# Two attention layers on one core: a head norm moved to DVE, another order in the first batches, and the last batch's value projections in the score banks

## What is computed

```python
def _L0_cond_ref(x, mask, Wq, Wo):
    q = jnp.transpose(x, (0, 2, 1)) @ Wq.T
    qh = q.reshape(B, T, NH, dk).transpose(0, 2, 1, 3)
    scores = scale * jnp.einsum('bhqd,bhkd->bhqk', qh, qh)
    logits = (scores * cmask + (1.0 - cmask) * NEG) * rmask
    ctx = jnp.einsum('bhqk,bhkd->bhqd', jax.nn.softmax(logits, axis=-1), qh)
    return jnp.transpose(ctx.transpose(0, 2, 1, 3).reshape(B, T, D) @ Wo.T, (0, 2, 1))
...
def _L1_cond_ref(x, emb, W_emb, b_emb, g_norm, W_qkv, g_q, g_k, W_out):
    scale, shift = jnp.split(emb @ W_emb + b_emb, 2, axis=-1)
    xn = _rms_norm(x, g_norm) * (1.0 + scale) + shift
    q, k, v = heads(xn @ W_qkv)
    q, k = _rms_norm(q, g_q), _rms_norm(k, g_k)
    attn = jax.nn.softmax(jnp.einsum('bhqd,bhkd->bhqk', q, k) * d ** (-0.5), axis=-1)
    o = merge(jnp.einsum('bhqk,bhkd->bhqd', attn, v))
    return o + o @ W_out
x = x + _L0_cond_ref(x, cond_2048, L0_cond_Wq, L0_cond_Wo)
x = x + _L1_cond_ref(x, cond_2048[:, None, :], ...)
```

## Time and profile before

| what | value |
|---|---|
| three runs, median (lowest to highest) | 1290.88 us (1289.24 to 1292.41) |
| the profiled execution, its own time | 1290.69 us |
| its span, first to last instruction | 1288.5 us |
| mean granted TensorE clock | 0.981 |
| busy: PE, DVE, POOL, ACT | 1231.0, 1032.1, 771.6, 768.5 us |

### The profile page before, as it was taken

One profiled execution on the slowest core, in us unless ns is written; L12 is line 12 of the kernel. 1 busy time (PEld: TensorE's weight loads), 2 busy tenths in 40 slices (PEclk: granted clock), 3 DMA queues, 4 the chain that ended last, 5 costly groups with the idle time before them and its releaser, 6 DMA issues.

```text
span 1288.5 us, 20732 instructions
## 1 busy us (share of the span) xinstructions
PE 1231.0 (96%) x6769; PEld 577.5 (45%) x6769; DVE 1032.1 (80%) x920; ACT 768.5 (60%) x1394; POOL 771.6 (60%) x387
## 2 busy tenths in 40 slices
PE   3889899999999999999999999999999999999998
PEld 1364444545444454544445454444544444454434
DVE  6666878788887878888787888878888897887664
ACT  1616566766656576665657656565766656566524
POOL 1517566484756748575574857557485755837542
PEclk7969999999999999999999999999999999999999
DMA  5712635435373543536354353635345363533432
GB/s 143 266 34 75 155 92 123 110 88 125 82 171 92 120 111 83 133 82 168 95 117 110 87 132 82 163 97 116 95 102 138 82 161 93 119 91 74 98 73 59
DMA packets 77975, 143.00 MB, mean 111 GB/s; under 512 B 21552, under 2 KB 23088, under 8 KB 77872
## 3 DMA queue, kind: packets, MB, share of 16 engines
q1 hardware_dynamic: 69552, 130.36, 40.5%
q10 hardware_dynamic: 8320, 11.32, 3.3%
HBM read 32.02 MB, written 8.39 MB: 31 GB/s over the span
## 4 chain that ended last, share of the span: by engine, by line
PE 80%; POOL 6%; DVE 4%; issue 3%; ACT 3%; SPq 2%; DMA 1%; ACTq 1%; DVEq 0%; POOLq 0%
PE PX L599 25%; PE PS L501 9%; PE PO L531 8%; PE PX L633 8%; PE PS L518 5%; PE PO L553 5%; POOL RQK L2272 4%; PE PM L464 4%; PE PX L570 2%; PE PM L570 2%; PE PO L556 2%; PE PM L473 2%; SPq L2453 2%; PE PM L542 1%; PE PM L581 1%
## 5 line engine op out<-in xcount | busy, mean ns | idle before, releaser
L1213 ACT ACTIVATE E<-PS,KBIAS 128x512 f32<-128x512 f32 x512 | 340.8, 686 | 195.8 <-PE PS L501 152.6
L599 PE MATMUL PX<-WQKV,XNT 128*128 128x512 f32 x752 | 377.2, 604 | 0.7 <-DVE XNT L1895 0.4
L1822 DVE TENSOR_REDUCE NM<-PM 128x4 f32<-128x2048 f32 x128 | 292.1, 2282 | 72.3 <-PE PM L464 72.3
L2260 POOL TENSOR_TENSOR E<-E 128x1024 f32<-128x1024 f32 x112 | 263.3, 2370 | 88.1 <-PE PO L531 77.8
L501 PE MATMUL PS<-B,A 97*128 97x512 f32 x512 | 287.5, 597 | 4.6 <-ACT E L1213 3.8
L2290 POOL TENSOR_TENSOR KQLO<-E 128x1024 f32<-128x1024 f32 x64 | 151.6, 2368 | 224.4 <-ACT E L1220 222.7
L2272 POOL TENSOR_TENSOR RQK<-RQK,HALF 128x16 f32<-128x16 f32 x64 | 212.8, 3331 | 94.7 <-DVE RQK L1910 94.3
L1220 ACT ACTIVATE E<-PS 128x512 f32<-128x512 f32 x256 | 146.9, 597 | 110.6 <-PE PS L518 110.4
L599 PEld LDWEIGHTS PX<-WQKV,XNT 128*128 128x128 f32 x752 | 134.0, 191 | 99.7 <-issue 89.7
L1829 DVE TENSOR_REDUCE NM<-PM 128x8 f32<-128x2048 f32 x64 | 146.3, 2286 | 37.1 <-PE PM L473 37.1
L501 PEld LDWEIGHTS PS<-B,A 97*128 97x128 f32 x512 | 92.2, 189 | 156.5 <-issue 105.2
(11 more groups left out here) (87 smaller groups left out, 1352.4 us busy)
## 6 DMA issues: line engine op xcount, KB each, us to landing
A<-KQHI SPq DMA_DIRECT2D x126, 128.0 KB, 2.4
B<-KQHI SPq DMA_DIRECT2D x126, 128.0 KB, 2.4
A<-QHI SPq DMA_DIRECT2D x248, 64.0 KB, 2.0
B<-QHI SPq DMA_DIRECT2D x248, 64.0 KB, 2.0
XB<-x SPq DMA_DIRECT2D x16, 512.0 KB, 4.1
X<-x ACTq DMA_DIRECT2D x16, 512.0 KB, 5.0
out<-X1R SPq DMA_DIRECT2D x32, 256.0 KB, 2.9
A<-KQLO SPq DMA_DIRECT2D x63, 128.0 KB, 2.4
```

The source lines that it names most:

```text
L599: last = mm(bank, XNT[:, c, t * P:(t + 1) * P], WQKV[:, c, part * DM:(part + 1) * DM], start=(c == 0), stop=(c == 3))
L1213: fn(E[:, probs(seg, i, g), h, :], PS[n % 2][:, :], ACT.Exp, bias=KBIAS[:, g, b:b + 1], scale=SCALE).then_inc(exp_done, 1)
L1822: v.tensor_reduce(NM0[:, q, :].rearrange("p (h k) -> p h k", k=KB0)[:, :, kb], PM[:, :, :], axis=AX.X, op=ALU.max, negate=True).then_inc(m ...
L2260: g_.tensor_tensor(running(seg, i)[:, heads_, :], running(seg, i)[:, heads_, :], E[:, probs(seg, i, g), heads_, :], ALU.add).then_inc(done, 1)
```

## The change

It has three parts. (1) In the steady iterations DVE does the norm of head block 1, between its fourth maximum of layer 0 and an add of exponentials; POOL's list loses it. (2) In the fill, TensorE computes batch 0's first two scores ahead of the second maxima group and the next batch's first projection behind the third; near its end the fourth maxima group of batch 1 goes ahead of the output projection, on TensorE and DVE; and the normalized rows are transposed ahead of batch 1's values, with ScalarE's modulation ahead of its value copy. (3) In iteration 16 the value projections go to the banks PS1 and PS0, counted by a new semaphore `values_taken`, and are spread between transposes and maxima; the rest of the output matmuls go between the scores. ScalarE copies both value tiles before the first exponential, and issues the second half of the maxima rows after two exponentials instead of four. DVE's second residual goes behind the last maximum.

```diff
@@ BIG[16], MAXES[0]
-            (("w1", 0), -2, 0), (("w1", 1), -2, 0), (("v1", 0), -1, 0), (("v1", 1), -1, 0)),
+            (("w1", 0), -2, 0), (("w1", 1), -2, 0)),
...
+        def last_values_bank(t):
+
+            return PS[SCORES.upto(("C", t), NB) % 2]
@@ score1
                 if b == NB - 1:
+                    if u < 2:
+                        pe.wait_ge(values_taken, u + 1)
@@ values_and_sums1
                 if c == 0:
-                    pe.wait_ge(big_taken, BIG.upto(("v1", 1), i))
+                    if b == NB - 1:
+                        pe.wait_ge(values_taken, 2)
+                    else:
+                        pe.wait_ge(big_taken, BIG.upto(("v1", 1), i))
@@ project1
-                bank = heads_bank(i - 1, k) if key[0] == "p1" else PX[:, :]
+                late = key[0] == "v1" and i == NB
+                bank = last_values_bank(t)[:, :] if late else heads_bank(i - 1, k) if key[0] == "p1" else PX[:, :]
                 if cs[0] == 0:
-                    if key[0] == "p1" and i == NB and k % 2:
+                    if late:
+                        pe.wait_ge(exp_done, SCORES.ahead(("C", 0), i))
+                    elif key[0] == "p1" and i == NB and k % 2:
@@ TensorE, iterations_0_and_1
                 maxima0(i, i, 1, 0)
+                score0("A", i, i, 0, 0, 0)
+                score0("A", i, i, 0, 0, 1)
                 maxima0(i, i, 1, 1)
-                score0("A", i, i, 0, 0, 0)
-                project0(i, i + 1, 0)
-                score0("A", i, i, 0, 0, 1)
                 values0(i, i, 0)
                 score0("A", i, i, 0, 0, 2)
                 score0("A", i, i, 0, 0, 3)
                 maxima0(i, i, 1, 2)
+                project0(i, i + 1, 0)
...
                 modulation(4)
+                maxima0(i, i + 1, 0, 3)
                 out0(i, i, 0)
                 out0(i, i, 1)
-                modulation(5)
-                maxima0(i, i + 1, 0, 3)
-                modulation(6, 7)
+                modulation(5, 6, 7)
                 rows0(i, i + 1, 0)
+                norm_rows(i, i)
                 values0(i + 1, i + 1, 0)
-                norm_rows(i, i)
@@ ScalarE, iteration_16
                 values1(i, i - 1, 0)
+                values1(i, i - 1, 1)
                 exp1(i, i - 1, 0, 0)
                 exp1(i, i - 1, 0, 1)
+                rows1_half(i, i - 1, 1)
                 exp1(i, i - 1, 0, 2)
                 exp1(i, i - 1, 0, 3)
-                rows1_half(i, i - 1, 1)
                 exp1(i, i - 1, 1, 0)
                 exp1(i, i - 1, 1, 1)
-                values1(i, i - 1, 1)
@@ DVE, iteration (steady)
                     maxima0(i, i, 1, 3)
+                if l1:
+                    norm_heads(i, i - 1, 1)
+                if l0:
                     add_keys0("A", i, 3, True)
@@ DVE, iteration_16
                 maxima1(i, i - 1, 0)
-                residual1(i, i - 2, 1)
                 maxima1(i, i - 1, 1)
                 maxima1(i, i - 1, 2)
                 maxima1(i, i - 1, 3)
+                residual1(i, i - 2, 1)
@@ POOL, iteration (steady)
                     power_heads(i, i - 1, 2)
-                    norm_heads(i, i - 1, 1)
                     norm_heads(i, i - 1, 2)
```

More of the change, by code:

```diff
@@ L162 @@
             (("t0", 1), 0, 3), (("n0", 1), 0, 0), (("s0", 0), 0, 3), (("q0", 0), 1, QUAD), (("s0", 1), 0, 3),
-            (("q0", 1), 1, QUAD), (("q0", 2), 1, QUAD), (("w0", 1), 0, 3), (("q0", 3), 1, QUAD), (("n0", 0), 1, 0),
-            (("t0", 0), 1, 0), (("t1", 0), 0, 1), (("t1", 1), 0, 2), (("t0", 1), 1, 3), (("q1", 0), 1, QUAD),
+            (("q0", 1), 1, QUAD), (("q0", 2), 1, QUAD), (("q0", 3), 1, QUAD), (("w0", 1), 0, 3), (("n0", 0), 1, 0),
+            (("t1", 0), 0, 1), (("t1", 1), 0, 2), (("t0", 0), 1, 0), (("t0", 1), 1, 3), (("q1", 0), 1, QUAD),
             (("q1", 1), 1, QUAD), (("q1", 2), 1, QUAD), (("q1", 3), 1, QUAD), (("n0", 1), 1, 0), (("tq", 0), 0, 1),
@@ L363, in cond_resid @@
         big_taken = sem("big_taken")
+        values_taken = sem("values_taken")
         def running(seg, i):
@@ L1134, in iteration_16 @@
                 heads_rows(i, i - 1, 1)
-                out1(i, i - 2, 0, 3)
+                values1(i, 0, 0)
                 heads_rows(i, i - 1, 2)
                 heads_rows(i, i - 1, 3)
-                out1(i, i - 2, 1, 0, 1)
+                out1(i, i - 2, 0, 3)
+                values1(i, 0, 1)
                 maxima1(i, i - 1, 0)
-                out1(i, i - 2, 1, 2, 3)
+                values1(i, 0, 2)
+                values1(i, 0, 3)
                 maxima1(i, i - 1, 1)
-                values1(i, 0, 0)
+                values1(i, 1, 0)
+                values1(i, 1, 1)
                 rows1_half(i, i - 1, 0)
                 maxima1(i, i - 1, 2)
-                values1(i, 0, 1, 2)
+                values1(i, 1, 2)
+                values1(i, 1, 3)
                 maxima1(i, i - 1, 3)
-                values1(i, 0, 3)
+                out1(i, i - 2, 1, 0, 1)
                 score1(i, i - 1, 0, 0)
                 score1(i, i - 1, 0, 1)
+                rows1_half(i, i - 1, 1)
                 score1(i, i - 1, 0, 2)
                 score1(i, i - 1, 0, 3)
-                rows1_half(i, i - 1, 1)
-                values1(i, 1, 0)
                 score1(i, i - 1, 1, 0)
                 score1(i, i - 1, 1, 1)
-                values1(i, 1, 1, 2, 3)
+                out1(i, i - 2, 1, 2)
                 score1(i, i - 1, 1, 2)
                 score1(i, i - 1, 1, 3)
+                out1(i, i - 2, 1, 3)
                 score1(i, i - 1, 2, 0)
@@ L1308, in values1 @@
                 act.wait_ge(visit_done, visit("C", i - 1, 3) if b > 0 else 0)
-                copy(V1[:, t, :], PX[:, :]).then_inc(big_taken, 1)
+                if b == NB - 1:
+                    copy(V1[:, t, :], last_values_bank(t)[:, :]).then_inc(values_taken, 1)
+                else:
+                    copy(V1[:, t, :], PX[:, :]).then_inc(big_taken, 1)
             def round_heads(i, b, k):
@@ L1561, in iterations_0_and_1 @@
                 rows0(i, i + 1, 0)
+                modulate(i, i)
                 values0(i + 1, i + 1, 0)
-                modulate(i, i)
                 exp0("A", i + 1, i + 1, 0, 0)
```

## The result

| | before | after |
|---|---|---|
| median of the runs, us | 1290.84 (1289.24 to 1292.41, 4 runs) | 1299.62 (1299.31 to 1302.93, 4 runs) |
| ratio | | 1.0063, 95% interval 1.0048 to 1.0079 |
| profiled execution: span, time, us | 1288.5, 1290.69 | 1297.5, 1299.32 |
| mean granted clock | 0.981 | 0.980 |

The account below looks back on a forecast made before the run. TensorE, busy 96%, was taken as the bound, with one steady wait of 0.8 us for POOL. Steady iterations 0, fill +1.1 and tail +4.3 gave +5.4 on 1290.69, so 1296.1 us; range 1291.5 to 1300.5.

Parts of the forecast that it names:

- One sign of being wrong: Steady iterations: the prediction would be wrong if an iteration differed from 75.5 us by more than 0.1.
- Part 1, cost 0: Steady iterations: DVE's new norm fills 0.58 us of idle before the add, leaving 0.2 to 0.3 to spare; gain 0.
- Rival 2: Steady iterations: DVE and POOL exclude each other, the new norm waits for the power's end; 27 us, 1323; chance 0.04.
- rival 3: Steady iterations: POOL's queue sets the stall, so the 0.8 us wait goes in all 13; -10.6, 1285.5; chance 0.07.
- Part 2, start, +2.0: Start of fill: TensorE stands empty 2.4 us, score (1,0) and full clock come later; +2.0, bounds +0.9 and +4.1.
- the first score needs the row DMA, landed 2.8 us later, so it starts at 30.8: Start of fill: row DMA issued at 27.99 lands 2.8 us later, and batch 0's first score starts then.
- Part 2, end, -0.9: End of fill: output projection later, but about 3.2 us leave the chain to the query-key projection; -0.9, bounds -1.6 and +0.8.
- up to 0.7 of the difference goes to the modulation coefficients: End of fill: the modulation coefficients, now late on DVE, take up to 0.7 us of the gain.
- Part 3, +4.3: Last batch: gain up to 3 us from moved value projections is outweighed by later waits; +4.3, bounds 3.2 and 6.9.
- (a): Last batch: DVE's residual waits for a later output matmul ahead of three splits, so the splits start 1.8 us later.
- (c): Last batch: copy to X1R waits for a later store, at 1272.7 instead of 1268.69; +4.0 for the exponentials behind it.
- (b): Last batch: ScalarE issues row DMAs (2.42 us) before two exponentials; exponential (1,3) ends at 1269.1, before by 1268.8.

Follow-up runs that it names:

- the fourth group: Copy to X1R two exponentials later in every steady iteration: on the kernel before 0.9999, on the changed kernel 1.0064, both against the kernel before.
- a_keep: The changed kernel with ScalarE's copy to X1R two exponentials later in every steady iteration: 1.0064 (1.0052 to 1.0076) against the kernel before, +8.3 us.

## Why the prediction was right, and where not

The forecast was +5.4 us and slower; +8.8 (6.2 to 10.2) came, inside the range and above the forecast by 3.4. It is inside with 0.9 us to spare, and partly by luck: alone, part 2 measures at the upper bound given for it (+4.0 of +4) and part 3 above its own (+7.2 of 6.9). One sign of being wrong appeared, iterations that differ from 75.5 by more than 0.1 (76.07, 76.38, 75.84); by the fourth group the loss does not hang on them.

**Part 1, cost 0: right, step by step.** The norm took 0.68 us, the add followed at once, the reciprocal ended at 347.59, and 0.31 us of slack were left where 0.2 to 0.3 had been worked out. Alone the part measures +0.3 (-1.0 to +1.7). Rival 2 (27 us) is out, by 0.68 us beside a running power; rival 3 (-10.6) is out, by a wait of L630 that is still 0.9 us at the longest and 13 times there.

**Part 2, start, +2.0: the mechanism was right, the size low.** TensorE stood empty 2.40 us ahead of the value transposes, as worked out, and score (1,0) came 1.9 us later against the first matmul. Full clock came at some 39.2 instead of 36.0, late as foreseen. Alone it measures +3.4 (1.8 to 4.8). The step "the first score needs the row DMA, landed 2.8 us later, so it starts at 30.8" took one landing for all. It came after 2.29 us of waiting here and after 1.11 to 3.51 elsewhere, and now the second maximum pays whatever it takes, 0 to 2.2 us. Before, this maximum did not stand behind the transfer.

**Part 2, end, -0.9: not seen; it is +0.1 (-1.4 to +1.8), which does not exclude -0.9.** The step that failed is "up to 0.7 of the difference goes to the modulation coefficients". The maximum that left the chain had kept DVE busy while POOL multiplied QF; with it gone, DVE's row norm starts 0.06 us after POOL's instruction and takes 1.49 us instead of 0.48, and the coefficients behind it hold ScalarE's modulation. That microsecond is as large as the gain that was forecast; that it is what ate the gain is argued, since no run keeps the new order and undoes the meeting.

**Part 3, +4.3: the mechanisms were right, the size low; +7.2 (5.6 to 8.9) alone.** (a) was +1.8 us at the splits: they came 1.83 later than in before from the first split on. (c) had the copy 3.6 us behind the end of exponential (1,3); it was 3.67. The step that was mis-sized is **(b)**, "exponential (1,3) ends at 1269.1, and by 1268.8 before": +0.3. From the first split it ended 28.54 us on (1274.27 - 1245.73) where before had 26.94 (1268.82 - 1241.88): **+1.6**. I had counted the issues as ScalarE's time and not followed TensorE, which stood 2.56 us and then ran at 0.51 of its clock from 1270 to 1275, so that ScalarE waited 0.46 and 1.48 us for its scores. Before's tail had more time at half clock, some 10 us against 7, but two thirds of that lay ahead of its first score; what counts is where it falls. The copy thus came +5.4 us late, not +4.0. The second size was the clock *behind* the copy's standstill: taken as 0.4, it was -0.3 in one profiled execution and +2.2 in another (16.44 and 18.90 us from the copy to the last residual, against 16.70).

**The sum.** The parts alone add up to 0.3 + 4.0 + 7.2 = 11.5, and the whole measures 8.8 (8.3 in `a_keep`). With half-widths of 1.4 to 1.8 us on each this is no contradiction; nor do the runs show that the parts help each other.

## What to carry to other kernels

A transfer or copy that waits for another engine's late store should stand behind everything it would hold up: one 1.06 us copy in the wrong place of ScalarE's list cost 5.4 us, some of it through TensorE's clock. When work is taken out of a wait to gain its time elsewhere, price the empty wait twice, once as time and once as TensorE's clock behind it, and follow each move on the engine that is *waited for* too. Moving an instruction behind a DMA makes it inherit the scatter of that DMA's landing.

## What the runs showed of the hardware

- DVE's row norm, one SBUF input and one SBUF output, was held up by a POOL multiplication that had started 0.06 us before: 1.49 us instead of 0.48, in all four profiled executions where they met, ending 0.28 to 0.29 us after POOL's instruction, which took its usual 1.26 to 1.27. DVE's head norm with two SBUF inputs took 0.68 us in the middle of POOL's powers, as fast as without (0.69 at 1241.27 in before, with POOL idle). By the Trainium skill ("SBUF — State Buffer", "Who interferes with whom") an operation of `tensor_scalar`'s kind can take the port pair that DVE shares with POOL, and the one that starts first holds it; the first pair of numbers agrees with that. By the same section a DVE instruction with two SBUF inputs contends with a POOL instruction that reads SBUF; the second pair does not show it.
- The same standstill of TensorE (2.39 to 2.49 us) in the same code was followed by clock 1.00 in two profiled executions and by a stretch at 0.50 in three (1280 to 1285 us, above).
- An issue of a stack transfer on SP, mostly 0.5 to 0.6 us, took 2.31 and 1.83 us in two iterations of the changed kernel, and 2.07 and 1.84 in two of before.
